# Layer 0 attention: turned probabilities copied between maxima, roots for two batches, outputs turned over two steps

## The reference

```
x = x + tanh(g_xattn[0]) * attention(layernorm(x), ctx)   # 16 heads of 16, mask True = left out
scores = sigmoid(layernorm(x) @ gate_w.T)                 # 8 experts
sel    = top_2(scores + expert_bias)
routed rows are scaled by their score and sent to their expert
```

## Time and profile before

| | |
|---|---|
| median of 3 runs | 1991.19 us (1990.56 to 1992.09) |
| the profiled execution | 1999.09 us, its span 1997.4 us |
| PE busy | 1740.5 us, 87% of the span |
| DVE busy | 1070.9 us, 54% |
| ACT busy | 776.4 us, 39% |
| POOL busy | 258.6 us, 13% |
| granted TensorE clock, mean | 0.941 |

### The profile page before, as it was taken

How to read it: one execution, slowest core, us unless ns; L and a number is a source line. 1 busy time by engine, 2 the same in 40 slices (tenths; PEclk the granted TensorE clock), 3 DMA queues, 4 the chain that set the end, 5 groups by cost and what they waited for, 6 DMA issues and landing times. The chain is left out here.

```text
span 1997.4 us, 28170 instructions
## 1 busy us (share of the span) xinstructions
PE 1740.5 (87%) x9431; PEld 1264.5 (63%) x9431; DVE 1070.9 (54%) x3135; ACT 776.4 (39%) x1785; POOL 258.6 (13%) x277
## 2 busy tenths in 40 slices
PE   6888658879989899999848689999979999999796
PEld 4656545656757567888737558888645665656563
DVE  4867655647667462323238554101346767676564
ACT  5777763355555311111125312221124444444321
POOL 2100112031020120000141130000040001010232
PEclk9988878989999899999969789999989999999898
DMA  7644003311111322545334558334222111110452
GB/s 230 218 141 156 32 13 110 88 55 38 33 54 54 116 90 93 178 149 168 119 118 143 188 184 281 128 111 136 99 76 75 41 41 51 30 48 12 130 160 77
DMA packets 170925, 212.91 MB, mean 107 GB/s; under 512 B 17081, under 2 KB 137506, under 8 KB 170658
## 3 DMA queue, kind: packets, MB, share of 16 engines
q1 hardware_dynamic: 159730, 183.57, 28.9%
q0 software_dynamic: 10496, 27.28, 4.3%
q10 hardware_dynamic: 560, 0.27, 0.0%
HBM read 148.95 MB, written 57.92 MB: 104 GB/s over the span
## 5 line engine op out<-in xcount | busy, mean ns | idle before, releaser
L761 POOL DMA_INDIRECT slots_in<-f_xn,f_slot x88 | 85.5, 971 | 501.8 <-DVE f_slot L538 478.0
L3459 PE MATMUL r_bank<-r_w,r_hT 128*128 x624 | 139.3, 379 | 1.0 <-DVE r_hT L3603 1.0
L3459 PEld LDWEIGHTS r_bank<-r_w,r_hT 128*128 128x128 f32 x624 | 118.4, 190 | 22.8 <-issue 7.5
L1321 PEld LDWEIGHTS a_t<-kept_ident,a_probs 128*128 128x128 f32 x768 | 83.9, 143 | 66.0 <-issue 42.5
L2239 DVE CUSTOM_DVE_ANT_0 a_s<-a_s,a_mask_bias 128x256 f32<-128x256 f32 x256 | 99.6, 461 | 44.1 <-PE a_s L2068 37.1
L1471 ACT ACTIVATE a_probs<-a_s,a_negmax 128x512 f32<-128x512 f32 x128 | 86.9, 684 | 92.4 <-DVE a_negmax L1720 92.3
L1305 PE MATMUL a_s<-a_kT,a_qT 64*128 64x256 f32 (+1 forms) x512 | 110.6, 531 | 10.7 <-ACT a_probs L1477 5.1
L3074 PE MATMUL r_bank<-r_xgT,r_firsts 128*128 128x256 f32 x512 | 113.2, 379 | 0.0
L1321 PE MATMUL a_t<-kept_ident,a_probs 128*128 128x128 f32 x768 | 107.3, 283 | 5.4 <-ACT a_probsT L1495 3.4
L1720 DVE TENSOR_REDUCE a_negmax<-a_s 128x1 f32<-128x512 f32 x128 | 82.2, 684 | 51.4 <-PE a_s L1305 48.3
L3544 DVE TENSOR_TENSOR r_y<-r_bank,r_b_row 128x256 f32<-128x256 f32 (+1 forms) x27 | 14.7, 544 | 177.1 <-PE r_bank L3459 176.5
(11 more groups left out here) (427 smaller groups left out, 3548.5 us busy)
## 6 DMA issues: line engine op xcount, KB each, us to landing
r_firsts<-in_f_w SPq DMA_DIRECT2D x27, 1024.0 KB, 5.1
r_firsts<-in_f_w SPq DMA_DIRECT2D x46, 512.0 KB, 4.4
slots_in<-a_zeros SPq DMA_DIRECT2D x8, 2048.0 KB
half_in<-a_zeros SPq DMA_DIRECT2D x8, 1024.0 KB
r_w<-in_f_w SPq DMA_DIRECT2D x8, 1024.0 KB
a_share_of<-shares_out SPq DMA_DIRECT2D x28, 256.0 KB, 3.9
r_xg<-slots_in SPq DMA_DIRECT2D x28, 256.0 KB, 3.5
slots_out<-r_y SPq DMA_DIRECT2D x28, 256.0 KB
```

Of the source, the lines that this page charges most:

```text
L761: pool.indirect_dma_start(self.slots_in[:, :], bass.IndirectOffsetOnAxis(ap=self.slot[:, c, tile:tile + 1], axis=0), src, None).then_inc(s ...
L1321: last = nc.tensor.transpose(bank[:, n * P:(n + 1) * P], src, ident[:, :])
L3459: last = nc.tensor.matmul(d_bank[:, t * D:(t + 1) * D], hT[:, j % 2, m, t * P:(t + 1) * P], slots.second[:, bass.ds(e, 1), m, :], start=(m ...
```

## The change

Four edits, all in the attention of layer 0:

- Which turned bank is copied by whom and when: `ACT_TURNS` is a tuple. Normally ACT copies banks 1 (between its exponents) and 2 (after them), DVE bank 0 (between maxima 1 and 2) and 3 (after them). In the steps of more_turns ACT still copies all four.
- Outputs are turned back over two steps, half 0 at u = 1 and half 1 at u = 2; o_raw has five slots in a ring, since the next batch's first block is copied meanwhile.
- The routing's roots are asked for two batches at once (0 and 1, 2 and 3, 4 and 5, then 6 alone), at steps 10, 18, 26 and 30, instead of at 6, 10, 14, ... 30. Two batches are then normed in one step and turned in one step; logits follow at steps 15, 16, 23, 24, 29 (two) and 33. ACT takes the square roots (those of x_stats too) in the next step, behind `move_heads` and before the exponents, instead of at the end of the asking step.
- The choice for batches 0 to 3 runs at steps 25 to 29 instead of 22 to 25; the one for 4 and 5 at 30 to 34 instead of 30 to 33. Its five parts are spread 2, 2, 1 over three steps. STEPS is 35.

```diff
@@ -429,6 +429,9 @@
 
     def vector_normed(self, dve, step, b):
         self.norm.scale(dve, step, b, b + 1)
+        self.vector_xn(dve, b)
+
+    def vector_xn(self, dve, b):
         if self.cfg.routed and b >= self.cfg.held:
             k = self.group_of[b - self.cfg.held]
             dve.wait_ge(self.scattered[k % 2], self.rows_sent(k))
@@ -1793,9 +1796,10 @@
     KT = SEQ // P
     VW = H * DV
     TURNS = GROUPS
+    OUTS = BLOCKS + 1
     LAG_T, LAG_PV = 1, 2
     RT = 4
-    BACK_AT = 1
+    BACK = {1: 0, 2: 1}
     STEPS_OF = BLOCKS * BATCH
     assert TURNS * 512 == GROUPS * KT * SEQ
 
@@ -1805,10 +1809,10 @@
         return [(kind, b + 1, n) for kind, n in PACKED_STEP[u]]
 
     def back_jobs(b, u):
-        return [("oback", b - 1, t) for t in range(TB)] if u == BACK_AT and 0 <= b - 1 < BATCH else []
+        return [("oback", b - 1, BACK[u])] if u in BACK and 0 <= b - 1 < BATCH else []
 
     def out_step(e):
-        return (e + 1) * BLOCKS + BACK_AT
+        return (e + 1) * BLOCKS + max(BACK)
 
     extra = defaultdict(list)
     for e in range(2, BATCH):
@@ -1817,18 +1821,22 @@
         extra[(e - 2) * BLOCKS].append(("x_stats", e, 0))
         extra[(e - 2) * BLOCKS + 1].append(("x_scale", e, 0))
     more_turns = set()
-    for b in range(route.cfg.last):
-        s = out_step(b) + 1
-        extra[s].append(("f_ask", b, 0))
-        extra[s + 1].append(("f_normed", b, 0))
-        extra[s + 2].append(("f_turn", b, 0))
-        extra[s + 3].append(("f_logits", b, 0))
+    SOON = route.choose_groups[-2][0]
+    for b0 in range(0, route.cfg.last, 2):
+        b1 = min(b0 + 2, route.cfg.last)
+        s = out_step(b1 - 1)
+        extra[s].append(("f_ask", b0, b1))
+        extra[s + 1].append(("f_scale", b0, b1))
+        for b in range(b0, b1):
+            extra[s + 1].append(("f_normed", b, 0))
+            extra[s + 2].append(("f_turn", b, 0))
+            extra[s + (3 if b >= SOON else 5 + b - b0)].append(("f_logits", b, 0))
     for k, (b0, b1) in enumerate(route.choose_groups[:-1]):
-        s = out_step(b1 - 1) + 5
+        s = out_step(b1 - 1) + (4 if b1 > SOON else 7)
         extra[s].append(("f_exp", b0, k))
-        extra[s + 1].append(("f_choose", b0, k))
-        extra[s + 2].append(("f_gates", b0, k))
-        extra[s + 3].append(("f_count", b0, k))
+        for n, parts in enumerate((2, 2, 1)):
+            extra[s + 1 + n].append(("f_choose", k, parts))
+        extra[s + 4].append(("f_count", b0, k))
         more_turns |= {s + 1, s + 2, s + 3}
     STEPS = max(max(extra), out_step(BATCH - 1)) + 1
 
@@ -1849,7 +1857,7 @@
         if weighed:
             number("o", *weighed)
         if turned:
-            ACT_TURNS[turned] = 4 if s in more_turns else 2
+            ACT_TURNS[turned] = (0, 1, 2, 3) if s in more_turns else (1, 2)
             for i in range(TURNS):
                 number("pT", turned, i)
         for kind, e, n in back_jobs(b, u) + prep_jobs(b, u):
@@ -1860,7 +1868,7 @@
 
     moved_at, freed_at = {}, {}
     for (kind, e, i), n in t_at.items():
-        by_scalar = kind in ("x", "q", "k", "o", "f_turn") or kind == "pT" and i < ACT_TURNS[e]
+        by_scalar = kind in ("x", "q", "k", "o", "f_turn") or kind == "pT" and i in ACT_TURNS[e]
         at = moved_at if by_scalar else freed_at
         at[n] = len(at)
 
@@ -1889,8 +1897,8 @@
         probsT = sb("probsT", [P, 2, GROUPS * KT, SEQ])
         negmax = sb("negmax", [P, 2, GROUPS, TB])
         exp_table = sb("exp_table", [P, 1])
-        rsums = sb("rsums", [P, TB, H])
-        o_raw = sb("o_raw", [P, BLOCKS, SEQ])
+        rsums = sb("rsums", [P, H])
+        o_raw = sb("o_raw", [P, OUTS, SEQ])
         o = sb("o", [P, VW])
         bqs = sb("bqs", [P, PACK, NC_])
         mask8 = sb("mask8", [P, TB, SEQ], U8)
@@ -2097,7 +2105,7 @@
                 bank = t_turn(t_at["oback", e, t])
                 for blk in range(BLOCKS):
                     last = nc.tensor.transpose(bank[:, blk * P:(blk + 1) * P],
-                                               o_raw[:, blk, t * P:(t + 1) * P], ident[:, :])
+                                               o_raw[:, (e * BLOCKS + blk) % OUTS, t * P:(t + 1) * P], ident[:, :])
                 last.then_inc(t_full, 1)
 
             pe.wait_ge(pre.landed, pre.total)
@@ -2165,7 +2173,7 @@
 
             def move_heads(e, u):
                 bank = full(act, t_at["o", e, u])
-                nc.scalar.copy(o_raw[:, u, :], bank[:, 0:SEQ]).then_inc(t_moved, 1)
+                nc.scalar.copy(o_raw[:, (e * BLOCKS + u) % OUTS, :], bank[:, 0:SEQ]).then_inc(t_moved, 1)
 
             move("k", 0)
             norm.take(act, 0, 2)
@@ -2175,29 +2183,31 @@
             for s in range(STEPS):
                 b, u = divmod(s, BLOCKS)
                 turned = block_of(s, LAG_T)
+                by_act = ACT_TURNS[turned] if turned else ()
                 if block_of(s, LAG_PV):
                     move_heads(*block_of(s, LAG_PV))
+                for kind, e, n in extra[s - 1]:
+                    if kind == "x_stats":
+                        norm.take(act, e, e + 2)
+                    elif kind == "f_ask":
+                        route.norm.take(act, e, n)
                 if b < BATCH:
                     exponent(b, u, 0)
                     exponent(b, u, 1)
-                if turned:
-                    move_turned(*turned, 0)
-                    move_turned(*turned, 1)
+                for i in by_act:
+                    if i < 2:
+                        move_turned(*turned, i)
                 if b < BATCH:
                     exponent(b, u, 2)
                     exponent(b, u, 3)
-                if turned:
-                    for i in range(2, ACT_TURNS[turned]):
+                for i in by_act:
+                    if i >= 2:
                         move_turned(*turned, i)
                 for kind, e, n in prep_jobs(b, u):
                     if kind != "v":
                         move(kind, e)
                 for kind, e, n in extra[s]:
-                    if kind == "x_stats":
-                        norm.take(act, e, e + 2)
-                    elif kind == "f_ask":
-                        route.norm.take(act, e, e + 1)
-                    elif kind == "f_turn":
+                    if kind == "f_turn":
                         route.scalar_turned(full(act, t_at[kind, e, n]), e).then_inc(t_moved, 1)
                     elif kind == "f_exp":
                         route.scalar_exp(act, n)
@@ -2255,9 +2265,9 @@
             def move_back(e, t):
                 n = t_at["oback", e, t]
                 heads = full(dve, n)[:, :].rearrange("p (h r) -> p h r", h=H)
-                step(nc.vector.reciprocal(rsums[:, t, :], heads[:, :, DV]))
+                step(nc.vector.reciprocal(rsums[:, :], heads[:, :, DV]))
                 nc.vector.tensor_tensor(o[:, :].rearrange("p (h d) -> p h d", h=H), heads[:, :, 0:DV],
-                                        rsums[:, t, :].unsqueeze(2).to_broadcast([P, H, DV]), ALU.mult).then_inc(t_free, 1)
+                                        rsums[:, :].unsqueeze(2).to_broadcast([P, H, DV]), ALU.mult).then_inc(t_free, 1)
                 taken(dve, n)
                 tile = e * TB + t
                 step(nc.vector.scalar_tensor_tensor(out=kept.x[:, tile, :], in0=o[:, :], scalar=tanh_g[:, cfg.layer:cfg.layer + 1],
@@ -2268,24 +2278,24 @@
 
             def route_job(kind, e, k):
                 if kind == "f_ask":
-                    route.norm.ask(step, e, e + 1)
+                    route.norm.ask(step, e, k)
+                elif kind == "f_scale":
+                    route.norm.scale(dve, step, e, k)
                 elif kind == "f_normed":
-                    route.vector_normed(dve, step, e)
+                    route.vector_xn(dve, e)
                 elif kind == "f_logits":
                     route.vector_logits(dve, step, full(dve, t_at[kind, e, k]), e)
                     dve.sem_inc(t_free, 1)
                 elif kind == "f_exp":
                     route.vector_ask(dve, step, k)
                 elif kind == "f_choose":
-                    if k == 0:
-                        dve.wait_ge(route.consts_in, 16 * len(route.consts))
-                        dve.wait_ge(kept.tables_in, 64)
-                    choices[k] = route.choose_parts(dve, step, k)
-                    for _ in range(3):
-                        next(choices[k])
-                elif kind == "f_gates":
-                    for _ in choices[k]:
-                        pass
+                    if e not in choices:
+                        if e == 0:
+                            dve.wait_ge(route.consts_in, 16 * len(route.consts))
+                            dve.wait_ge(kept.tables_in, 64)
+                        choices[e] = route.choose_parts(dve, step, e)
+                    for _ in range(k):
+                        next(choices[e], None)
                 elif kind == "f_count":
```

(14 more changed lines are left out.)

## The result

The changed kernel takes 1970.04 us (median, 1966.72 to 1973.31), the kernel before in the same rounds 1991.64 (1990.56 to 1992.82). The ratio is 0.9898 with a 95% interval of 0.9874 to 0.9922: faster by 21.6 us. The forecast was 1971.5.

The account below looks back on a forecast made before the run. Layer 0's attention was taken as bound by a ring of waits between ACT, PE and DVE. Terms -13.7 - 0.4 - 7.1 + 1.5 = -19.7 from the median 1991.2 gave 1971.5 us, range 1960 to 1984.

Parts of the forecast that it names:

- steps 2 to 22: Attention of layer 0: plain steps, queries, loads, turns, logits, clock and outputs sum to 148.2 us from 161.9, or -13.7.
- steps 22 to 31: End of layer 0's attention, with group 0's choice and scatter: 78.0 without the stall of 9.9, or -7.1 us.
- tail: After step 31: last outputs, count and scaled rows in step 34 move group 1's first transfer back by 1.5 us.
- Copies between maxima: Plain attention steps: DVE's copy 0 fits between maxima with 0.15 to spare; a step takes 6.12 instead of 6.6 us.
- Rival (b): Plain step doesn't shorten because copy 0 holds maximum 3: 1977.6 with half the gain lost, 1983.7 with all; chance 0.14.
- Outputs over two steps: DVE's lateness after output steps goes, 3.0 us in all; four steps with a query projection become 0.85 longer than plain.
- Roots: Square-root table loads: three of ten pairs go; the remaining ones, behind the heads, count in full at 2.76 us each.
- Logits: Logits on PE fall on steps with a projection, 0.9 us each; 1.8 for steps 15 and 16.
- The clock: PE at half clock after table loads: 1.8 us for each of four loads between 2 and 22, 7.2 in sum.
- Rival (c): Each of seven loads and four late steps costs a whole step at half clock, 4.6 us: 2010; chance 0.09.
- The stall I kept at 9.9: ACT's wait of 9.90 us for heads while POOL issues group 0's scatter: same size, moved with the scatter.
- Rival (a): The stall at group 0's scatter goes, 1961.6, chance 0.12; or up to doubles, 1981.4, chance 0.05.

Follow-up runs that it names:

- twice-read run: Changed kernel with one more DVE maximum over bank 0 ahead of its copy; 1889.46 us, ratio 0.9896 to the kernel before on chip B.
- roots behind the step: Changed kernel with ACT taking square roots at the end of the asking step, before the heads; 1877.75 us, ratio 0.9840 to the kernel before on chip A.
- roots shared: Changed kernel with x statistics of batches 4 and 6 moved to steps 10 and 18, sharing the routing root's load; 1872.23 us, ratio 0.9804 on chip B.
- roots alone: Changed kernel with the copies and outputs put back as before; 1902.58 us, ratio 0.9968 to the kernel before on chip A.
- late scatter: Changed kernel with POOL's scatter of group 0 issued in step 34 instead of 29; 1884.86 us, ratio 0.9877 to the kernel before on chip B.

## Why the prediction was right

- **The stage.** Measured from first exponents: steps 0 to 2 14.56 (forecast 14.3), steps 2 to 22 144.78 (148.2), steps 22 to 31 87.43 (87.9), tail +1.0 (+1.5); at group 1's first transfer -23.6 in place of -19.7. The medians differ by 21.6.
- **Copies between maxima**: right in mechanism and size. A plain step is 6.05 to 6.16 (6.12 forecast), ACT waits for no maximum in it, and 0.13 is spare by the twice-read run (0.15). Rival (b) is out.
- **Outputs over two steps**: DVE's lateness in 5, 13 and 21 is gone. The price in the query step was mis-sized: 6.57 is 0.5 over plain, not 0.85, in each of the four steps counted. Copy 1 stands behind four exponents alone and frees its bank 4.54 after the scores (64.77 + 0.61 - 60.84), where I had 4.95; the projection waits 0.20, not 0.4. Step 2 has a query but no output to turn, and costs nothing over plain without the low clock (6.06 with roots behind the step, 6.05 with roots shared; its 6.80 here is clock).
- **Roots**: the interval of a pair that went fell from 9.25 to 6.60 with the roots alone, as forecast. One that stays costs 2.93 at step 8 (8.99 against 6.06), where I had 2.76; 82.23 to 85.04 is 2.81 from load to exponents. The Trainium skill (ScalarE: Activation LUTs, What ACT_TABLE_LOAD costs) gives 2.66 for one switch, so near 5.3 for a pair of them. The runs show about half. What I took as given, that roots stand behind the heads at full price, was the change's weak point: behind the step four of them cost 0.9 to 1.4 less.
- **Logits**: 0.43 in intervals 15 and 23 (6.49 against 6.06), not 0.9: I counted the length of a merged run, not what it adds.
- **The clock**: of four drops between 2 and 22 at 1.8, that in 11 is missing (6.15), that in 19 is 1.4 (7.50), those in 9 and 17 are 1.8: 5.0. Not counted were 0.7 in interval 2, 0.65 in interval 10 (10.15 where 18, with the same work, is 9.50; its turns at 92.50 are at half clock) and 0.1 in 20: 6.5 in all in place of 7.2.
- **What 2 to 22 missed by**, 3.4 but for rounding: queries 1.4, plain steps 20 x 0.06 = 1.2, logits 0.9, clock 0.7 and output steps 0.1, against loads that cost 0.7 more (2.93 four times) and turns 0.1. Errors of both signs stood in it. Rival (c), a whole step at half clock after each load, did not come. The Trainium skill (TensorE: Matmul & The Clock Gate, Part 1) has idling lower the clock. The changed kernel's trace agrees in that between 2 and 22 the clock fell only behind a load; but it did not fall behind each, as interval 11 shows. With two loads gone it was full over 100 to 200 us (1.00).
- **22 to 31**: the sum is right, the terms are not. 27 is 12.07 against 10.5 and 28 is 8.14 against 6.6. The 3.77 that ACT waits for DVE in step 28 is the lateness that I had put at 3.9, and not the clock's doing. The clock's part is in the value projection, which runs at half clock behind the load's gap. In the twice-read kernel it runs at full clock, ACT waits 3.75 all the same, and interval 27 is 10.49, as forecast. The changed kernel's rows, then those of the twice-read one (PE's and ACT's timelines):

```profile
220.84 3.54 PE L2054 MATMUL a_t<-kept_weights,a_c_turned 128*128 128x256 f32 x8 [3.56 <-ACT a_probsT L2172]
```
```profile
230.72 1.60 ACT L2165 ACTIVATE a_probs<-a_s,a_negmax 128x256 f32<-128x256 f32 x4 [3.77 <-DVE a_negmax L2249]
```
```profile
226.63 1.97 PE L2055 MATMUL a_t<-kept_weights,a_c_turned 128*128 128x256 f32 x8 [3.56 <-ACT a_probsT L2173]
```
```profile
234.93 1.60 ACT L2166 ACTIVATE a_probs<-a_s,a_negmax 128x256 f32<-128x256 f32 x4 [3.75 <-DVE a_negmax L2250]
```

  The stall I kept at 9.9 and moved: it moved, and became 13.77; that it would stay near its size was an assumption, not a reading. Interval 30 is 9.04 without it (late scatter, chip B) and 21.14 with it, so it cost 12.1 instead of 9.9. The low clock came to 3.1 in 27 and 28, where 4 was counted, and intervals 22 to 25 to 25.63 instead of 27.2, by the same query and logits terms. With 0.4 less in 29 and 0.2 more in 26 and 30 the errors cancel to 0.5 under the forecast, which is luck.
- **Rival (a)**, the stall gone or doubled: on the first chip and on C it is there and 1.4 to 1.6 times as long, on A and B no traced kernel has it.
- **Beyond the stage**: I counted 0. In the profile POOL's transfers are 23.6 earlier at group 1, 22.2 at the stage's last group (318.98) and 28.4 late in the span (1419.53); on C 26.75 at group 1 and 20.9 late (1432.46). So the later layers give or take some 6 us, and the agreement of 1971.5 with 1970.04 is closer than the parts warrant: the mechanism of the stage was right, the last 2 us are luck.

What made PE's signals late stays open. No run here varied the transfers' size or number with the rest unchanged, and putting the scatter off was run on a chip without stalls.

## What to carry to other kernels

In a ring of engines that each walk a written order, a copy can be priced by its place in the queue more than by its length: the same DVE copies cost no wait of ACT in plain steps between the maxima and 9 us over the stage behind them. Put a table load where the engine waits anyway, and let roots of different owners share one pair (here the second was worth more, and left little to the first); look for idle time of TensorE next to it, since the step after may pay again in clock. Parts of a change can need each other in some steps though their times seem to add, so compare step by step in the trace, and compare only kernels run on the same chip.

## What was unexpected of the hardware

- The unchanged kernel took 1908.39, 1909.22, 1991.64 and 1995.81 on four chips, up to 4.6% apart. On the two slower ones DVE, ACT and PE stall while POOL issues indirect transfers, up to 16.1 us at once; whether that is the chip itself is not shown.
- A drop of the clock did not follow from the length of the idle stretch just before: PE is at full and at half clock after the same 2.79 and after the same 3.56 (226.63 with bank 0 read twice, 220.84), and scores are at full and at half clock after the same 0.75 (60.84 and, in the step behind a root, 88.61). Two load pairs less gave back 5 us in clock besides 5.8 in loads.
